# A four-stage transformer program as one block: stages overlapped, autocorrelation over three iterations, first feed-forward in tile pairs

## What is computed

```python
# stage 1, "ac": autocorrelation attention, 8 heads, per batch and column
corr = ifft(fft(q) * conj(fft(k))).real
topk = int(2 * log(256))                      # 11
w, idx = top_k(corr over time, topk); w = softmax(w)
out = sum_i w_i * v[min(idx_i + pos, L - 1)]
x = x + tanh(g_xattn[0]) * out                # k = v = ctx
# stage 2, "f0": dense layer plus a LoRA branch of rank 8, 16, 32 or 64, chosen per token
out = h @ W.T + b
sel = argmax(h @ gate_w.T + gate_b)
x = x + tanh(g_ffn[0]) * (out + h @ A[:r].T @ B[:, :r].T)
# stage 3, "at": attention, 32 query heads, 8 key/value heads of 128, rope, mask
x = x + tanh(g_xattn[1]) * (softmax(q k.T / sqrt(128)) v) @ wo
# stage 4, "f1": dense layer whose weight is W_base plus a Fourier-transformed low-rank update
x = x + tanh(g_ffn[1]) * (h @ (W_base + update).T + b_base)
```

## Time and profile before

| what | value |
|---|---|
| three runs | 3479.38 to 3483.66 us, median 3482.95 us |
| the profiled execution, its own time | 3481.08 us |
| its span, first to last instruction | 3479.3 us |
| PE busy | 3228.4 us, 93% |
| DVE busy | 2029.5 us, 58% |
| ACT busy | 1126.8 us, 32% |
| POOL busy | 614.5 us, 18% |
| TensorE clock granted, mean over the span | 0.961 of full |

### The profile page before, as it was taken

How to read it: one execution, slowest core, us unless ns; L and a number is a source line. 1 busy time by engine, 2 the same in 40 slices (tenths; PEclk the granted TensorE clock), 3 DMA queues, 4 the chain that set the end, 5 groups by cost and what they waited for, 6 DMA issues and landing times. The chain is left out here.

```text
span 3479.3 us, 43167 instructions
## 1 busy us (share of the span) xinstructions
PE 3228.4 (93%) x15536; PEld 2660.2 (76%) x15536; DVE 2029.5 (58%) x4835; ACT 1126.8 (32%) x2345; POOL 614.5 (18%) x504
## 2 busy tenths in 40 slices
PE   9999699996899958999789999999999999999799
PEld 7888577774667747888678888788887788888687
DVE  4322588996333337777566666766666666666432
ACT  4111455553111124444333332333332333333211
POOL 2322344452111112333210000000000000000122
PEclk9999899997899979999899999999999999999899
DMA  6332211112222145676556545445454464543321
GB/s 225 121 121 103 87 38 72 66 44 98 79 87 92 72 169 188 230 242 229 171 184 238 167 156 174 171 151 200 157 170 164 158 218 158 170 157 131 149 85 67
DMA packets 228406, 500.91 MB, mean 144 GB/s; under 512 B 22906, under 2 KB 57850, under 8 KB 228194
## 3 DMA queue, kind: packets, MB, share of 16 engines
q1 hardware_dynamic: 225490, 493.74, 41.1%
q10 hardware_dynamic: 2704, 4.41, 0.4%
HBM read 359.67 MB, written 138.41 MB: 143 GB/s over the span
## 5 line engine op out<-in xcount | busy, mean ns | idle before, releaser
L195 PE MATMUL PB<-at_woh,at_ah 128*128 128x512 f32 x1024 | 411.2, 402 | 4.9 <-POOL at_wol L183 3.4
L195 PE MATMUL PB<-at_hh,at_wqh 128*128 128x512 f32 x1024 | 402.7, 393 | 2.7 <-DVE at_hl L183 1.5
L195 PE MATMUL PB<-at_hl,at_wqh 128*128 128x512 f32 x1024 | 401.5, 392 | 0.0
L195 PE MATMUL PB<-at_hh,at_wql 128*128 128x512 f32 x1024 | 400.3, 391 | 0.0
L195 PE MATMUL PB<-at_woh,at_al 128*128 128x512 f32 x1024 | 399.8, 390 | 0.0
L972 ACT ACTIVATE at_ss<-at_ss,at_sm,at_bs 128x256 f32<-128x256 f32 x512 | 301.6, 590 | 302.4 <-DVE at_sm L970 302.4
L195 PE MATMUL PB<-at_wol,at_ah 128*128 128x512 f32 x1024 | 399.5, 390 | 0.0
L939 DVE TENSOR_TENSOR at_t<-PB,at_rt 128x512 f32<-128x512 f32 x128 | 88.5, 691 | 451.8 <-PE PB L195 451.8
L1026 DVE SCALAR_TENSOR_TENSOR at_xt<-PB,gt,at_xt 128x512 f32<-128x512 f32 x256 | 190.6, 747 | 121.1 <-PE PB L195 121.1
L180 ACT ACTIVATE at_ah<-PB 128x512 fp32r<-128x512 f32 x128 | 76.6, 599 | 493.4 <-PE PB L195 493.4
L195 PEld LDWEIGHTS PB<-at_hh,at_wqh 128*128 128x128 f32 x1024 | 194.4, 190 | 40.4 <-issue 3.2
(11 more groups left out here) (246 smaller groups left out, 7344.0 us busy)
## 6 DMA issues: line engine op xcount, KB each, us to landing
at_wqh<-wqd SPq DMA_DIRECT2D x96, 512.0 KB, 3.7
at_wql<-wqd SPq DMA_DIRECT2D x96, 512.0 KB, 4.6
at_woh<-wod SPq DMA_DIRECT2D x48, 1024.0 KB, 5.2
at_wol<-wod SPq DMA_DIRECT2D x48, 1024.0 KB, 7.6
at_raw<-in_wq SPq DMA_DIRECT2D x32, 512.0 KB, 6.3
wqd<-at_wqh SPq DMA_DIRECT2D x32, 512.0 KB, 7.7
wqd<-at_wql SPq DMA_DIRECT2D x32, 512.0 KB, 8.1
at_raw<-in_wo SPq DMA_DIRECT2D x32, 512.0 KB, 6.4
```

Source lines behind the costliest of these rows:

```text
L195: e.matmul(o, a, b, start=i == 0, stop=last), *(waits if i == 0 else ()), *w, mark=last)
```

## The change

The whole program becomes one block. Each tile gets a fixed place in SBUF by hand (`place`), stages become generators that are advanced in turn, and where a stage reuses the place of another it waits for `q.now()`, the state of all engine counters at that point of the code. Parts that matter, shortened:

```diff
+        def now(self):
+            return tuple((e, self.count[e]) for e in self.ENG[1:])
...
-                    one_by_one(val_ops, vals_out, range(4), 0)
                     if tb < 3:
+                        one_by_one(val_ops, vals_out, range(4), 0)
                         side_by_side(val_ops, vals_out, range(4, 8), 4, renew)
-                    else:
-                        one_by_one(val_ops, vals_out, range(4, 8), 4)
...
-            q.run()
+            yield
+            for hf in range(2):
+                for tt in range(4):
+                    one_by_one(val_ops, vals_out, [2 * tt + hf], 4 + tt % 2)
+                    yield
...
-                    d["sp"] += split(sh[:, i, :], sl[:, i, :], pa[:, i, :], (d["sum"][i - 4],) + pf)
+                    d["sp"] += split(sh[i], sl[i], pa[i], (d["sum"][i - 4],) + pf, l_on="vector" if i == 4 else "gpsimd")
...
-                s_ = [op("vector", lambda e, k=k: e.scalar_tensor_tensor(
-                    out=w0[:, k, :], in0=w2[:, k, :], scalar=NEG, in1=w1[:, k, :], op0=ALU.is_equal, op1=ALU.mult,
-                    accum_out=t[k][:, 25:26]), r[k], x_[k]) for k in V4]
-                i_ = op("vector", lambda e: e.reciprocal(small(26), small(25)), s_[3])
-                d["W"] = tuple(op("scalar", lambda e, k=k: e.activation(
-                    w1[:, k, :], w0[:, k, :], ACT.Copy, scale=t[k][:, 26:27]), i_) for k in V4)
+                g = op("scalar", lambda e: e.activation(te[:, :, 0:TOPK], te[:, :, 0:TOPK], ACT.Exp), f)
+                h = op("vector", lambda e: e.tensor_reduce(tz[:, 1, :], te[:, :, 0:TOPK], AX, ALU.add), g)
+                h = op("vector", lambda e: e.reciprocal(tz[:, 2, :], tz[:, 1, :]), h)
+                s_ = [op("vector", lambda e, k=k: e.tensor_scalar(w0[:, k, :], w2[:, k, :], NEG, tz[:, 2, k:k + 1], ALU.is_equal, ALU.mult), r[k], h)
+                      for k in V4]
+                d["W"] = tuple(op("gpsimd", lambda e, k=k: e.tensor_tensor(w1[:, k, :], w1[:, k, :], w0[:, k, :], ALU.mult), s_[k], x_[k])
+                               for k in V4)
...
+            def split_W(u, js):
+                for j in js:
+                    d["spW"] += split(sh[j], sl[j], pa[j], (d["sumW"][j],) + pf, l_on="vector" if j == 0 else "gpsimd")
...
-            for u in range(NU + 1):
+            for v in range(NU + 2):
+                a, b, c = v, v - 1, v - 2
+                if a < NU:
+                    P1(a)
+                if 0 <= b < NU:
+                    weights(b)
...
+                if a < NU:
+                    P1b(a)
...
+                if c >= 0:
+                    P5(c, 0)
+                    finish(c, 0)
+                    P5(c, 1, 0)
+                if 0 <= b < NU:
+                    P3(b)
+                if c >= 0:
+                    P5(c, 1, 1)
...
+                if 0 <= b < NU:
+                    P4(b)
+                    split_W(b, (0, 1))
+                if a < NU:
+                    P2(a)
+                    rows(a)
```

In the first feed-forward `lora_in` serves two tiles at once (24 float32r matmuls of 256 columns for a pair, with the small weight as the stationary operand), the LoRA part of a tile is 4 matmuls instead of 6, the first two tiles' 96 matmuls run chunk by chunk as the weight arrives, and `second_weight` uses the places of the raw weight, leaves the weight already split, so that "f1" only loads it:

```diff
+            for c in range(2, C):
+                if c + 2 < C:
+                    split_w(c + 2, *room["rest"])
+                for t in range(2):
+                    for hf in range(2):
+                        product(t, hf, [c])
...
+                    lds = [dma(f"co{x_}", co[:, :, x_, :], coef[x_].rearrange("(c p) r -> p c r", p=P), *ws[5]) for x_ in range(3)]
...
+        next(kv)
+        next(ac)
+        for _ in range(4):
+            next(kv)
+        next(ac)
+        for _ in range(2):
+            next(kv)
+        next(ac)
+        for _ in kv:
+            pass
...
+        next(ac)
+        f0.send(q.now())
+        next(ac)
+        f0.send(stored["ac"])
+        for _ in ac:
+            pass
+        f0.send(q.now() + stored["x"][6] + stored["x"][7])
...
+        for t in f0:
+            if t == 8:
+                next(at_)
...
+        for _ in range(4):
+            f1.send(q.now())
+            next(at_, None)
+        for _ in at_:
+            pass
+        f1.send(q.now())
+        q.run()
```

936 lines of the change are left out of this document (574 added, 362 removed).

## The result

The changed kernel takes 3355.61 us (median of 4 runs, 3351.99 to 3356.54). The kernel before, timed beside it, took 3482.75; the ratio is 0.9635, with a 95% interval of 0.9618 to 0.9651. So the change is worth 127 us, and the forecast of 203 was 76 us too hopeful: 3355.6 lies outside 3235 to 3335. The profiled execution took 3351.99 us with a span of 3350.2, against 3481.08 and 3479.3.

The account below looks back on a forecast made before the run. PE was taken as the bound, about 3,076 us of work in a 3479.3 us span; work -41 and stretches -37, -11, -43, -18, -34, -18, -1 sum to -203, giving 3280 us, range 3235 to 3335.

Parts of the forecast that it names:

- Work: PE's own work: cheaper LoRA input, fewer LoRA matmuls, 16 more transposes; together -41 us.
- "kv" to "ac": End of "kv" to second unit of "ac": excess 36 to 25 us, PE waiting 14 (0 to 16) behind ACT's prologue.
- Units of "ac": Twelve units of "ac": 24.5 us each, DVE about 21, POOL 21.8; excess 48 to 11 us, -37.
- first rival: "ac": moving to POOL wins nothing, a unit stays at 27.6 us; 3330 us, chance 0.13.
- End of "ac" to "f0": Last units, drain and start of "f0": loads and norms move between units; excess 64 to 21 us, -43.
- The coefficients: First tile pair of "f0": DVE waits for coefficient loads ahead of tile 2's remainders; 8 us taken, 3 to 20 possible.
- "f0": "f0" itself: one input for two tiles halves hand-overs to DVE; excess 41 to 23 us, -18.
- Start of attention: Transposes and norms leave the seam, PE waits about 15 us with DVE behind the mask; excess 69 to 35, -34.
- Body of attention: Attention's main loop: same loop, excess stays 94 us, change 0.
- "f1": Seam to "f1": weight, first tiles, transposes ready, tile 2's norm about 5 us late; excess 24 to 6, -18.
- queues in order give the seams back: Rival: loads heading ACT's or DVE's queue hold PE at coefficients, first seam, mask, "f1"; 30 us, 3310 us, chance 0.17.
- The rule against the change: DVE and POOL exclude each other on SBUF ports, so moving work may not help; forecast sided against it.

Follow-up runs that it names:

- e1: Changed kernel with the autocorrelation prologue's splits and statistics two value groups later, its transfers unmoved; 3335.2 us, ratio 0.9587.
- e13: Changed kernel with the next batch's layer norm statistics issued behind the splits of the next context tile, not in front; 3343.2 us, ratio 0.9619.
- e5: Changed kernel with one more of a unit's six remainders on DVE in place of POOL; 3364.8 us, ratio 0.9686.
- e10: Changed kernel with the peaks' maximum subtraction and sum moved from DVE into ACT's exps; 3344.2 us, ratio 0.9619.
- e15: Changed kernel, three iterations kept, with all six remainders of a unit on DVE; 3390.7 us, ratio 0.9744.
- e7: Changed kernel with every PE piece of the second weight's building two steps later; 3356.3 us, ratio 0.9652.
- e14: Changed kernel with PE's pieces of the second weight two steps later, and DVE's sum of the coefficients with them; 3351.7 us, ratio 0.9639.
- e2: Changed kernel with the first flips of the attention's hidden tile one tile pair later, loads and norms unmoved; 3343.0 us, ratio 0.9618.
- e4: Changed kernel with the attention mask's transfer issued first and its arithmetic behind the second query head's rope; 3341.7 us, ratio 0.9614.
- e3: Changed kernel with tiles 2 and 3 of the last feed-forward loaded and normalised earlier, with tiles 0 and 1; 3339.4 us, ratio 0.9602.
- e18: e17 with the first remainder of a unit's products on POOL too; 3313.8 us, ratio 0.9537.
- e17: Changed kernel with six edits: late prologue, later flip, early norms, mask first, peaks' exps and sums on ACT, statistics behind context splits; 3298.2 us, ratio 0.9489.
- e6: Changed kernel without POOL's four weight products: DVE's comparison multiplies with the exponentials, ACT scales by the reciprocal; 3377.8 us, ratio 0.9718.

## Why the prediction was wrong

Step by step, with the forecast's own terms:

- **Work**: 41 forecast, 39.5 by the records. Right, and the new LoRA rows of 256 columns start 0.118 us apart (24 from 822.64 to 825.36 us), where 0.119 was taken.
- **"kv" to "ac"**: the wait was named in place, engine and cause (ACT in front of `kv_oh`, two banks of cover) and came as 19.0 us where 14 was taken, outside the bound of 16. Its terms, one by one: the tables were issued 5.9 us after PE's last key product and not 5; ACT's prologue took 20.3 us (321.4 to 341.7) and not the old 22.2; and 3.7 us were left out, in which the first value output still goes through ACT and, behind the tables, DVE. Less the 10.9 us of cover that makes 19.0. The 2 us taken off for fewer bytes in flight are about what the prologue lost, though `x` came later: DVE waited for it until 332.9 us, 11.4 us after the tables were issued. The stretch saved nothing at all; e1 shows that 18 us were to be had at the first P4, and 14.6 at the end.
- **Units of "ac"**: 24.5 us was right for the short units (24.1) and wrong for the long ones (27.6). The step that failed is the mean: "about 21 us a unit" on DVE hid that the statistics fall into every second unit, where DVE has 3.1 us more and POOL's `ac_cl` stands behind them. Here twelve units took 14.5 us more than forecast. e13 shows order as a cause (the long unit 0.8 us shorter with no work moved); for DVE's load speak e5 (1 us longer with a remainder more) and, more weakly, e10. The prices were off too: the product became a comparison of 591 ns, no cheaper than the 495 and 79 of read-out that it replaced, where 0.1 less each was forecast; the small operations, taken as 0.4 us, hold a subtraction of 44 peaks of 880 ns and a sum of 190; a remainder on DVE took 1105, not 941. That makes 0.5, 0.7 and 0.3 us a unit, most of the 1.9 by which DVE is over its 21. A product on POOL took 770, not 650, inside its bounds. The first rival's unit of 27.6 us came in the long ones alone, and e15 puts it out: the move won 35 us.
- **End of "ac" to "f0"**: 21 forecast, 41 measured. The drain's 4.5 and 5 came as 3.45 before P4, 1.2 before P3 and 1.2 before P5; what was left out are the splits of the first flips (5.0 us), of the first weights (4.2) and of tiles 2 and 3 (2.0 and 5.6). The coefficients, taken as 8 us, were no cause: their six transfers were issued in 1.7 and 3.1 us for three each (the long issues of the earlier trace rows did not come), and e7 and e14 show that with them later the wait stays.
- **"f0"**: 23 forecast, 32 measured. "PE has a tile's products to cover each" failed at one place, where the first flip stands straight behind its norm's load: 12.7 us. e2 took it away, with 6 us of new waits for it. Another 5.4 us in two waits are on DVE's copy of the second weight (L1028); no run touches them.
- **Start of attention**: 35 forecast, 35.8 measured; the wait and its place as forecast (15 us: 15.6). The cause is only half of it: DVE waited 7.25 us for the mask, not 11, and e4, which takes the mask out of the way, leaves 9.0 of the 15.6 us, behind 7.3 us of ACT for a query weight that the forecast did not have. That the sum came out is luck.
- **Body of attention**: 94 forecast, 92.7.
- **"f1"**: 6 forecast, 26.6 measured. "Weight, first tiles and transposes are there" was true, and tile 2's norm was the right culprit, but it came as 10.1 us and not 5. Left out were a wait in the attention's tail and the lower clock (0.82). Of that tail's waits 1.5 us on `at_al` are as before; 4.6 us on `at_ptl` are new, and once more the head of a queue. ACT stands 7.2 us in front of the norm of a first tile of "f1", whose statistics wait for their transfer, with the attention's `at_pth` behind it at 3116.58:

```profile
3113.99 1.24 ACT L220 ACTIVATE f1xn<-f1xt,f1st 128x1024 f32<-128x1024 f32 x1 [7.17 <-POOL f1st L219]
```

No run takes this one away: e3 keeps it (4.4 us).

The mean of it: the forecast was close to right on what each engine has to do, and it took each seam at its first wait. The rival "queues in order give the seams back" was the right one in kind, but it was priced at 30 us. Of its four places the first seam and "f1" counted, the mask's wait was shorter than the forecast already had it, and the coefficients did not count; it lacked the flip in "f0" and the unit's head of queue.

The rule against the change: DVE's instructions with two SBUF sources did stretch, 941 to 1105 ns, while its products out of PSUM stayed at 673 to 677. The Trainium skill (SBUF — State Buffer, "SBUF: two separate sides") calls the port pair an exclusive lock, and here the trace agrees in size too. The subtraction of 44 peaks shows it best, since its place against POOL's work differs from kernel to kernel. First it, in the changed kernel, and what POOL does at that time, then it in e15, where POOL is idle there:

```profile
509.04 0.88 DVE L512 TENSOR_TENSOR ac_te<-ac_t 128x44 f32<-128x44 f32 x1
...
508.55 1.30 POOL L197 TENSOR_TENSOR ac_slw<-ac_paw,ac_shw 128x512 fp32r<-128x512 f32 x1
...
521.99 0.20 DVE L512 TENSOR_TENSOR ac_te<-ac_t 128x44 f32<-128x44 f32 x1
```

It takes 203 to 207 ns in all 16 units of e15 and 878 as a median in the change: it ends 0.07 us behind POOL's instruction, as if it had been held until shortly before that one's end. The remainders do the same: 676 ns at the least, 1105 beside a sum of POOL, and 7.35 us in e18 beside six of POOL's instructions. So DVE's waiting for POOL is inside its busy time. That DVE and POOL were busy 275.4 + 262.1 = 537 us in 310 therefore does not speak against the rule, and neither did the forecast's 466 in 331.6; what does speak against a full exclusion are the products out of PSUM, which run beside POOL unstretched. An estimate from these rows: in a unit of the change the subtraction loses 0.7 us, two remainders 0.9 and four comparisons (354 ns as a median over all 16 units, 591 as a mean in the twelve) 0.9, 2.5 us of DVE's 22.9; before the change six remainders lost 1.6 and four masked products (418 ns as a median, 495 as a mean) 0.3. So the change added about half a microsecond of such waiting a unit, and the rule did not cost the gain.

Open is the drain: 20 us over the forecast stand there, no run cured any of it, and e17's 3298 against the forecast's 3280 is about that size. Whether the splits of the first flips could run earlier was not tried, nor whether another order of DVE and POOL in a unit would keep their two-source instructions apart.

## What to carry to other kernels

Where stages overlap in one program with in-order queues, cost a seam by listing, for each engine, the first instruction that waits on a transfer and everything issued behind it, and look for the second wait behind the first: here issuing the same work in another order was worth 37 us by the ratio and 42 by the span over four places, about as much as the whole move of remainders to POOL (35 to 39). Do not take a mean over units that differ: what decides is the unit in which a periodic extra step falls. And a move to an idle engine and a deeper pipeline may be one change and not two: here the move without the third iteration costs 28 us. And where two engines hold each other up, an instruction's busy time contains its wait: compare its duration with the same instruction where the other engine is idle, before its load is called work.

## What was not expected of the hardware

- The wait of 19.0 us cost more than itself: with it the granted clock of 315.4 to 421 us was 0.84 as a mean, and 0.94 without it, and taking it away for a new one of 2.6 bought 18.4 us at the first P4, 2 more than the waits. Only 14.6 are left at the end: 3 went in "f0", in one execution of each kernel.
- A DVE subtraction of 44 columns took 204 ns where POOL was idle and 880 beside a POOL instruction, and a remainder of 512 columns 0.68 us alone, 1.1 beside one POOL instruction and 7.35 behind six in a row. Elsewhere DVE got its turn after one or two; why not there, no run shows.
- A comparison of 256 columns, with one SBUF source, took 346 to 839 ns, 591 as a mean, with POOL's products running beside it. In e6, where they are gone, an instruction with a third operand took 412 ns as a mean; the masked product of the kernel before took 412 to 1064, 418 as a median. How much of a mean is waiting is told by the shortest of the same instruction, not by another one.
- Four exps of 11 columns with a running sum took ACT 289 + 187 ns each, 1.9 us a unit, to spare DVE 1.07, of which 0.68 was waiting.
